# Down basis product in eight cell classes: half-height array tiles in two banks, put together by 0/1 products

## The reference, cut to what matters

```python
x = x + xattn(layernorm(x), ctx, Wq, bq, Wk, bk)       # q, k from ctx; energy = q k^T; softmax; x_m = x_n attn^T
gate_w, up_w = spline(gate_cp, 2048, 512), spline(up_cp, 2048, 512)
down_w = spline(down_cp, 512, 2048)                    # Catmull-Rom over out*in samples, 1/128.9 as many control points
inter = silu(layernorm(x) @ gate_w.T) * (layernorm(x) @ up_w.T)
x = x + inter @ down_w.T                               # x: (4, 512, 512), ctx: (4, 512, 256)
```

## Time and profile before

| | us |
|---|---|
| time, median of 3 runs (lowest, highest) | 282.28 (281.56, 283.15) |
| the profiled execution: its time, and its span | 281.58, 279.6 |
| PE busy | 261.1 |
| DVE, POOL, ACT busy | 182.0, 131.2, 124.5 |

### The profile page before, as it was taken

How to read it: one execution, slowest core, us unless ns; L and a number is a source line. 1 busy time by engine, 2 the same in 40 slices (tenths; PEclk the granted TensorE clock), 3 DMA queues, 4 the chain that set the end, 5 groups by cost and what they waited for, 6 DMA issues and landing times.

```text
span 279.6 us, 3824 instructions
## 1 busy us (share of the span) xinstructions
PE 261.1 (93%) x1250; PEld 170.2 (61%) x1252; DVE 182.0 (65%) x322; ACT 124.5 (45%) x202; POOL 131.2 (47%) x138
## 2 busy tenths in 40 slices
PE   7799469987999999999999999999999999599995
PEld 3223157853754858876638588756475889285674
DVE  0698986789567783864658837646597476574413
ACT  3034624215777712255866313468674132363300
POOL 0597443469771822307808223169174131495800
PEclk9968959999999999999999999999999999999999
DMA  6899034000550000022800000117000001100003
GB/s 202 308 426 407 13 117 187 0 0 2 165 212 0 2 1 0 2 100 71 354 0 0 0 0 0 75 75 300 0 0 0 0 0 75 75 0 2 0 0 150
DMA packets 7209, 23.23 MB, mean 83 GB/s; under 512 B 1184, under 2 KB 2336, under 8 KB 5792
## 3 DMA queue, kind: packets, MB, share of 16 engines
q1 hardware_dynamic: 7200, 23.11, 21.9%
HBM read 18.92 MB, written 4.19 MB: 83 GB/s over the span
## 4 chain that ended last, share of the span: by engine, by line
PE 79%; DVE 10%; ACT 4%; DMA 2%; issue 2%; POOL 1%; SPq 1%; DVEq 0%; ACTq 0%; POOLq 0%
PE bank L1304 12%; PE bank L1323 10%; PE bank L1349 10%; PE bank L1305 10%; PE bank L1157 5%; PE bank L1254 5%; PE bank L1256 5%; PE bank L1255 5%; PE bank L1168 4%; DVE prod L856 4%; PE bank L1356 3%; PE bank L1211 3%; DMA power<-in_g_power 2%; PE bank L1269 1%; SPq L579 1%
## 5 line engine op out<-in xcount | busy, mean ns | idle before, releaser
L1107 POOL TENSOR_TENSOR ih<-inter,ones 128x512 fp32r<-128x512 f32 x64 | 65.0, 1041 | 30.8 <-DVE inter L947 30.2
L947 DVE TENSOR_TENSOR inter<-inter,bank 128x512 f32<-128x512 f32 x64 | 43.4, 685 | 20.2 <-ACT inter L762 18.2
L762 ACT ACTIVATE inter<-bank 128x512 f32<-128x512 f32 x64 | 37.8, 601 | 17.7 <-PE bank L1305 17.6
L733 ACT ACTIVATE qk<-bank,nmr,rstd 128x512 f32<-128x512 f32 x16 | 12.5, 780 | 47.7 <-PE bank L1256 47.7
L1349 PEld LDWEIGHTS bank<-d_r,ih 128*128 128x128 f32 x256 | 30.6, 192 | 4.2 <-issue 3.2
L1304 PE MATMUL bank<-xh,gate_r 128*128 128x512 f32 x64 | 29.9, 467 | 1.5 <-DVE zg L939 1.5
L1349 PE MATMUL bank<-d_r,ih 128*128 128x192 f32 x256 | 31.1, 274 | 0.0
L1323 PE MATMUL bank<-inter,d_u 128*64 128x512 f32 x128 | 30.1, 602 | 0.0
L1304 PE MATMUL bank<-xh,up_r 128*128 128x512 f32 x64 | 26.0, 406 | 0.0
L1091 POOL TENSOR_TENSOR xres<-x,ones 128x2048 f32<-128x2048 f32 x4 | 14.4, 3601 | 23.9 <-DMA out<-xres 23.6
L1305 PE MATMUL bank<-zg,gate_v 102*128 102x512 f32 x64 | 25.4, 396 | 0.0
(11 more groups left out here) (100 smaller groups left out, 451.8 us busy)
## 6 DMA issues: line engine op xcount, KB each, us to landing
x<-in_x SPq DMA_DIRECT2D x4, 1024.0 KB, 4.8
xT<-in_xT SPq DMA_DIRECT2D x4, 1024.0 KB, 7.1
out<-xres SPq DMA_DIRECT2D x16, 256.0 KB, 2.1
ctxT<-in_ctxT SPq DMA_DIRECT2D x4, 512.0 KB, 7.5
rd<-in_d_r SPq DMA_DIRECT2D x2, 768.0 KB, 6.3
knots<-in_d_knot SPq DMA_DIRECT2D x1, 1280.0 KB, 12.7
d_coef<-in_d_coef SPq DMA_DIRECT2D x1, 1024.0 KB, 16.4
d_pt<-in_d_node SPq DMA_DIRECT2D x1, 1024.0 KB, 18.0
```

The lines of the kernel that those rows point to most:

```text
L762: nc.scalar.activation(inter[:, m], gbank[m % 2][:], ACT.Silu).then_inc(s["silu_done"], 1)
L947: V.tensor_tensor(inter[:, m], inter[:, m], ubank[m % 2][:], ALU.mult).then_inc(s["mult_done"], 1)
L1107: G.tensor_tensor(ih[:, m], inter[:, m], ones[:, 0].broadcast_to([P, TOK]), ALU.mult).then_inc(s["ih_done"], 1)
```

## The change

The 64 nodes are now dealt to eight classes (`D_CLS = 8`), with new cell edges so that each class meets each tile in exactly 64 rows. A tile's upper 64 rows hold class `w`, its lower 64 rows class `w + 4`. So each half tile needs 32 functions only, and `down_basis` issues two products for a tile, each of 64 rows and 32 columns: the upper half into quarter `w` of `zgbank`, the lower half into the same quarter of `zdbank`. `ORDER` goes through the four `w` in turn, so that eight products in a row are for eight different parts of the array. The two banks are copied out (`half_split`, ACT and DVE, into `zd` and `zp`) and put together by four 0/1 products (`gather_halves`), and `down_split` copies that sum to `zd`. The steps `odd_split`, `odd_place` are gone. The four energies of a batch in the loop go to four banks with nothing in between (`ebank`), and the last product of `gate_up(b, 9, a)` waits for all four exponentials, since `down_basis` reuses two of these banks.

```diff
-D_LIVE = 64
+D_LIVE = 32
+D_CLS = 2 * CLS
+NODE_ROWS = P // D_CLS
-ORDER = [CLS * w + a for pair in ((1, 3), (0, 2)) for a in range(CLS) for w in pair]
+ORDER = [CLS * w + a for a in range(CLS) for w in (1, 3, 0, 2)]
...
+        def ebank(b, t):
+            return abank[t % 2] if first(b) else (abank[0], abank[1], zdbank, zgbank)[t]
...
             if a is not None:
-                for t in range(2):
+                for t in range(NT):
                     st.energy(a, t)
                     st.softmax(a, t)
             st.gate_up(b, 8)
-            if a is not None:
-                st.energy(a, 2)
-                st.softmax(a, 2)
-            st.gate_up(b, 9)
-            if a is not None:
-                st.energy(a, 3)
-                st.softmax(a, 3)
+            st.gate_up(b, 9, a)
             st.down_basis(b, 0)
...
             st.gate_up(b, 10)
-            st.odd_split(b)
...
             st.down(b, 0, range(0, 12))
             st.down_basis(b, 1)
-            st.odd_place(b)
+            st.down(b, 0, range(12, 13))
             st.down_basis(b, 2)
-            st.down(b, 0, range(12, 16))
+            st.half_split(b)
+            st.down(b, 0, range(13, 16))
             st.down(b, 1, range(0, 16))
             if a is not None:
                 st.stats(a)
-                for t in range(3):
+                st.xm(a, 0)
+            st.gather_halves(b)
+            if a is not None:
+                for t in range(1, 3):
                     st.xm(a, t)
                 st.mean_shift(a)
-                for t in range(2):
-                    st.add_xm(a, t)
+                st.add_xm(a, 0)
             st.down_split(b)
...
 SP    +load(gather_in[:]..., "d_gather", "gather_in")      # 128 KB, ahead of knots; d_u is 256 KB now, was 512
 PE:
                         mm(dst[m % 2][:], gu_r[n][:, c, w * P:(w + 1) * P], xn2r[:, c], start=True, stop=False)
+                        if n == 1 and a is not None:
+                            pe.wait_ge(s["exp_done"], NT * (a + 1))
...
                 def down_basis(b, g):
-                    pe.wait_ge(s["mult_done"], MT * b + GROUPS[g][-1] + 1)
-                    dst = basis_bank[g > 0]
                     for m in GROUPS[g]:
-                        half = slice(m % 2 * HALF, (m % 2 + 1) * HALF)
-                        last = mm(dst[half], d_u[:, ORDER[m]], inter[:, m], ...)
+                        w = ORDER[m] // CLS
+                        for h, dst in enumerate((zgbank, zdbank)):
+                            part = slice(HALF * h, HALF * (h + 1))
+                            last = mm(dst[QUAD * w:QUAD * (w + 1)], d_u[part, ORDER[m]], inter[part, m], ...)
...
+                def gather_halves(b):
+                    pe.wait_ge(s["half_done"], 2 * b + 2)
+                    for h, halves in enumerate((zd, zp)):
+                        for z in range(2):
+                            last = mm(zgbank[:], gather[:, h], halves[:, z], ...)
 ACT:
+                def half_split(b):
+                    act.wait_ge(s["basis_mm"], len(GROUPS) * (b + 1))
+                    nc.scalar.activation(zd[:, 0], zgbank[:], ACT.Copy).then_inc(s["half_hi"], 1)
+                    nc.scalar.activation(zp[:, 0], zdbank[:], ACT.Copy).then_inc(s["half_hi"], 1)
```

More of the change, by code:

```diff
@@ L119, in gate_layout @@
     hidden = np.lexsort(((wrap + SHIFT * PERIOD / P) % PERIOD, cell % CLS))
[L120 to L123, removed]
+    down = (np.searchsorted(D_EDGES, np.arange(INTER), side="right") - 1) % D_CLS
+    if (np.bincount(CLS * down + cls) != HALF).any():
+        raise ValueError("no equal half tiles")
+    half = [[np.flatnonzero((cls == a) & (down == w)) for w in range(D_CLS)] for a in range(CLS)]
+    rows = np.stack([[np.append(half[a][w], half[a][w + CLS]) for w in range(CLS)] for a in range(CLS)])
     knot = np.rint(start + (offset + turn) * STEP).astype(np.int64)
@@ L212, in constants @@
         placed[:, row.ravel()] = full
-        basis[:, m] = np.concatenate([placed[:, QUAD * q:QUAD * (q + 1)] for q in (w, (w + 1) % CLS)], 1)
+        for h in range(2):
+            part = slice(HALF * h, HALF * (h + 1))
+            basis[part, m] = np.concatenate([placed[part, NODE_ROWS * (q % D_CLS):NODE_ROWS * (q % D_CLS + 1)] for q in range(w + CLS * h, w + CLS * h + 2)], 1)
         if not np.isclose(basis[:, m].sum(), full.sum()):
@@ L254, in xattn_spline_ffn_kernel @@
         d_u = sb("d_u", [P, MT, D_LIVE], f32)
-        turn = sb("turn", [P, P], f32r)
+        gather, gather_in = sb("gather", [P, 2, P], f32r), sb("gather_in", [P, 2, P], f32)
         ctxT = sb("ctxT", [P, CTX // P, TOK], f32)
@@ L1097, in replicate, with gate_up @@
                     pass
-                def gate_up(b, m):
+                def gate_up(b, m, a=None):
                     pass
@@ L1110, in down_basis, with half_split, gather_halves @@
                     pass
-                def odd_split(b):
+                def half_split(b):
                     pass
-                def odd_place(b):
+                def gather_halves(b):
                     pass
@@ L1313, in down_basis, with half_split, gather_halves @@
                 def down_basis(b, g):
-                    if g == 0:
-                        pe.wait_ge(s["dbasis_in"], 16)
-                    if g == 1:
-                        pe.wait_ge(s["zd_done"], b)
-                    pe.wait_ge(s["mult_done"], MT * b + GROUPS[g][-1] + 1)
-                    dst = basis_bank[g > 0]
                     for m in GROUPS[g]:
-                        half = slice(m % 2 * HALF, (m % 2 + 1) * HALF)
-                        last = mm(dst[half], d_u[:, ORDER[m]], inter[:, m], start=m % (MT // 2) < 2, stop=m % (MT // 2) >= MT // 2 - 2, skip_group_check=True)
+                        w = ORDER[m] // CLS
+                        for h, dst in enumerate((zgbank, zdbank)):
+                            part = slice(HALF * h, HALF * (h + 1))
+                            last = mm(dst[QUAD * w:QUAD * (w + 1)], d_u[part, ORDER[m]], inter[part, m], start=m < CLS, stop=m >= MT - CLS, skip_group_check=True)
                     last.then_inc(s["basis_mm"], 1)
-                def odd_split(b):
+                def half_split(b):
                     pass
-                def odd_place(b):
-                    pe.wait_ge(s["turn_set"], 2)
-                    pe.wait_ge(s["odd_done"], b + 1)
-                    for z in range(2):
-                        mm(zdbank[:], turn_[:], zd[:, z], start=False, stop=False, skip_group_check=True)
+                def gather_halves(b):
+                    pe.wait_ge(s["gather_set"], 1)
+                    pe.wait_ge(s["half_done"], 2 * b + 2)
+                    for h, halves in enumerate((zd, zp)):
+                        for z in range(2):
+                            last = mm(zgbank[:], gather[:, h], halves[:, z], start=(h, z) == (0, 0), stop=(h, z) == (1, 1))
+                    last.then_inc(s["gathered"], 1)
                 def down_split(b):
```

80 lines of the change are left out of this document (42 added, 38 removed).

## The result

| | before | after | ratio (95%) |
|---|---|---|---|
| run beside each other, us | 281.92 (281.28 to 283.15, 4 runs) | 271.39 (270.78 to 271.57, 4 runs) | 0.9628 (0.9601 to 0.9656) |
| profiled execution: time, span | 281.58, 279.6 | 271.57, 269.8 | |
| the same changed kernel again | 281.61 (17 runs) | 270.71 (269.14 to 272.33, 6 runs) | 0.9613 (0.9579 to 0.9646) |

The change makes the kernel 3.7% faster. The forecast was 270.0 us (268.0 to 273.8). The median came down by 10.5 us, the profiled span by 9.8, where the sum of the prediction had 12.3.

The account below looks back on a forecast made before the run. PE, busy for 93% of the span, was taken as the bound. Three loop batches saving 3.14 us each, plus 3.00 in the last, less 0.1, gave 12.3 us: 270.0 us from the median 282.28, range 268.0 to 273.8.

Parts of the forecast that it names:

- Do eight parts run side by side in rounds of 0.43?: Basis products on PE: claimed eight at once, 0.43 us a round; first block 1.87 us instead of 3.59; chance 0.74.
- Rivals 1 and 2: Basis products: row halves run one after the other, 283.7 us, chance 0.07; rounds longer than 0.43, 273.0 us, chance 0.08.
- rival 1: Basis products: the two row halves run one after the other, 1.4 us slower, 283.7 us; chance 0.07.
- The rule on weight loads: Basis rounds: loads overlap only products in different row groups; would gain 4.5 us more; given no chance.
- The estimate from that page's 10.6 for 16 parts: Basis rounds: a round would be 0.65 us and the kernel would take 277.
- Groups 1 and 2 and the product between them: Two later basis blocks with one `down` product between: 4.40 us before, 2.20 saved a batch.
- Gathering: Four added `f32r` products joining the halves: 0.92 us lost a batch, nothing hides it, its wait costs 0.
- The stall behind group 0: PE's wait at the second pair of `gate_up(10)`, after the first basis block: goes, 0.14 us saved.
- Energies and the wait: From first energy to basis: 5.4 us after, 5.48 before; wait 0.05 us, cost 0 in sum, bounds -0.1 and +0.4.
- `xm(2)`: Where PE needs ACT's `add_xm(0)`, which now waits for `nmr`: slack 0.9 us, cost 0.
- Prelude: Start of the kernel: 128 KB more loaded ahead of the knots, 0.1 us lost, of 0 to 0.3.
- Last batch: Batch after the loop, with no softmax and no such wait: 3.00 us saved; gathering just fits.

Follow-up runs that it names:

- pair_order: Changed kernel with the old order of tiles, so that consecutive basis products fall on four parts of the array, not eight; 284.44 us.
- banks_first: Changed kernel with energies 0 and 1 in the two banks the basis reuses, so the wait is for two exponentials, not four; 270.77 us.
- old_energies: Changed kernel with the energies as before: two banks, energies 2 and 3 behind gate_up 8 and 9, no added wait for the exponentials; 277.31 us.
- fill_last: Changed kernel with two f32 products, results unused, in PE's two waits of the last batch, before and after replicate; 268.67 us.
- fill_banks: Changed kernel with both fill_last's unused products in the last batch and banks_first's placing of the energies; 268.62 us.
- halves_outer: Changed kernel with each group's upper-half basis products issued first and its lower-half ones behind them; 270.48 us.
- new_energies_only: Kernel before with the energies' change alone (four banks, together, the wait for four exponentials), basis as it was; 280.52 us.
- again: The changed kernel itself, unaltered, measured and profiled once more; 270.71 us.
- all_three: fill_banks with the load of the gathering matrix moved from the head of SP's queue to its end; 269.02 us.

## Why the prediction was right, and where it was off

- **Do eight parts run side by side in rounds of 0.43?** Yes. Group 0 took 1.88 us (1.87), groups 1 and 2 1.02 each (1.01). Rivals 1 and 2 are out: 3.6 and 2.5 us would have shown them. pair_order shows the other side of the same sum, 0.43 a round with half the parts, and its whole time, 284.44 us, is near rival 1's price of 283.7, with 1.5 us of the clock in it.
- **The rule on weight loads** that the prediction weighed, from the Trainium skill ("TensorE: Matmul & The Clock Gate", Part 3, The mechanism), is not what the runs show; the same section also lets a load go ahead into the background weight buffer, which the prediction left out. In group 0, 16 products with 32-column loads in only two row groups leave 0.15 us beside their four rounds. The estimate from that page's 10.6 for 16 parts, 0.65 us a round, isn't seen either: with eight parts the rounds stayed at 0.43. No run here used 16 parts.
- **Groups 1 and 2 and the product between them**: 150.82 to 153.14, 2.32 us where before it was 4.40; with the product that leaves the list behind, 2.20 saved, as forecast. Gathering 0.92, no wait: as forecast.
- **The stall behind group 0** went (0.58 instead of 0.71), and DVE's product of tile 8 is through at 142.16 (141.47 and 0.69), 0.31 ahead of the product of PE that needs it (142.47).
- **Energies and the wait: the mis-sized term.** Forecast 5.4 us and 0 in sum; it was 5.63 where it had been 5.48, +0.15, inside its bounds of -0.1 and +0.4. The exponentials were done 5.15 us after the first energy, 0.03 later than forecast. What the prediction mis-sized is the price: PE stood 0.12 at the wait, and the record behind it was 0.1 longer than one that follows in a stream. banks_first, with the wait gone, has the 5.40. A turn thus is 1.71 + 0.14 + 2.20 - 0.92 - 0.15 = 2.98, measured 3.01.
- **`xm(2)`**: ACT's first `add_xm` waits for `nmr`, in all three turns (17.0 us together), and PE doesn't wait: right, by sign and size.
- **Prelude.** +0.1 forecast, +0.56 measured. The load isn't the cause: with and without it the starts lie on one line to 0.1 us, and moving it brought nothing that could be measured. The two profiles that are compared differ in where the first half-clock stretch lies (16.25 and 15.56), and by the table such a difference goes with the missing 0.5 us. That is an accident of these two executions, and neither a merit nor a fault of the prediction.
- **Last batch: the term that wasn't there.** The step of the sum that failed is "the last batch ... 3.00". All its parts were right, as old_energies, fill_last and fill_banks show, whose last batches take 38.53 to 38.56 us, 2.9 less than before. But the prediction took the clock of 1.00 as given there. The changed kernel gets 1.2 GHz for 3.4 us behind PE's two waits and loses 1.5 us, as the pair changed kernel and fill_last shows. The sum of the prediction has no term for the clock at all.

Together: 0.13 three times, 0.46 and 1.65 make the 2.5 us. The time lay in the stated range with 1.4 us above the forecast, and the mechanism held: this was not luck.

**What stays open**: why the clock fell behind two waits of 1.53 and 1.47 us in the changed kernel and not behind the same two in the kernel before. It fell in all five profiles of kernels with the new energies, the half tiles and no work in the waits (the changed kernel twice, pair_order, banks_first, halves_outer), where it starts 0.0 to 0.6 us after the second wait has ended, and in none of before, new_energies_only and old_energies, whose waits are as long to 0.01 us. Neither the length of the waits nor PE's list around them tells these apart. In old_energies three turns with the same list and the same wait gave a fall twice and none once. What does differ is when the waits come: the half-clock stretches of the start lie at another place against the instructions in each profile, and from the first of them to the end of the second wait it is 217.8 to 218.4 us in four of the five with the fall, 228.7 in pair_order, 227.3, 227.4 and 224.0 in before, new_energies_only and old_energies. So the theory put down ahead of `again`, that the fall depends on where the waits fall in time, is still open, since no run was made for it, and so is the possibility that the kernel before kept its clock by chance and loses it in some executions: of its 17 beside `again` four have a mean clock of 0.968 to 0.970, the others 0.973 to 0.976. That work in the waits keeps the clock is shown (fill_last, fill_banks, all_three); how long a wait may be is not. No run moved the waits alone.

## What to carry to other kernels

Where PE is the bound and a weight matrix has zero blocks, cut the product into array parts and deal the work so that consecutive products always fall on all parts: the number of parts in use sets the time (1.88 against 3.57 us for the same 32 records), not the number of products or their order inside a group. When a step on the bounding engine gets shorter, ask again what it covered; here the softmax had to move with it, or 6.6 of 10.9 us would have been lost, by the profiles some 5.5 of it to the new wait (three turns of 1.8) and most of the rest to the clock. And for PE's own waits look at the granted clock behind them, not at the wait alone: two waits of 1.5 us cost another 1.5 us after they were over, and two products without a use took that back at no cost. Whether such a loss comes can differ from one execution to another, so one profile on each side doesn't price it.

## What the runs showed of the hardware

- Eight parts of 64 rows and 32 columns run at the full rate of each: f32 rounds of 0.43 us and 0.15 us a block (1.88 us for four rounds, 1.02 for two).
- Products for busy parts don't block those for free parts behind them, over at least the four products (eight records) that stand between in halves_outer (group 0 took 1.90 us, where I had expected 2.73 if they did).
- A half-clock stretch came after a single wait of 1.62 us too (old_energies, 89.21 and 147.23, 1.3 and 1.8 us after its end), in two turns of three with the same list.
- The first half-clock stretch lies up to 3 us apart from one execution to another (14.49 to 17.53) and the loop's start up to 2.3. Among the six runs of the changed kernel the fastest, 269.14, has a mean granted clock of 0.973 and the slowest, 272.33, one of 0.956; that this is the cause of the spread is argued from these, not shown.
